# Rank counts placed ahead of a stage's first unit, and seven value tiles halved on VectorE before TensorE sums them

## The reference, cut to what matters

```python
scores = jnp.einsum('tbhd,sbhd->bhts', q, k) * scale     # t, s run over 8 rows
attn = jax.nn.softmax(scores, axis=-1)
ctx = jnp.einsum('bhts,sbhd->tbhd', attn, v)
attn_out = ctx @ out_w.T + out_b
```

```python
position_in_expert = jnp.cumsum(expert_mask, axis=0) - 1
expert_mask = expert_mask * (position_in_expert < capacity)      # capacity 320
...
hidden = jax.nn.silu(xf @ w_gate.T)
combine = (topk_gates[:, :, None] * one_hot(topk_idx)).sum(axis=1)
for e in range(8):
    y = y + combine[:, e:e + 1] * (hidden @ w_down[e].T)
```

## Time and profile before

| | us |
|---|---|
| median of 3 runs | 967.86 |
| lowest and highest | 961.92, 969.95 |
| the profiled execution's own time | 968.87 |
| its span, first to last instruction | 966.7 |
| PE busy in it | 784.6 |
| DVE busy in it | 630.6 |

### The profile page before, as it was taken

How to read it: one execution, slowest core, us unless ns; L and a number is a source line. 1 busy time by engine, 2 the same in 40 slices (tenths; PEclk the granted TensorE clock), 3 DMA queues, 4 the chain that set the end, 5 groups by cost and what they waited for, 6 DMA issues and landing times. The chain is left out here.

```text
span 966.7 us, 14811 instructions
## 1 busy us (share of the span) xinstructions
PE 784.6 (81%) x5019; PEld 536.6 (56%) x5019; DVE 630.6 (65%) x1795; ACT 406.5 (42%) x891; POOL 366.3 (38%) x514
## 2 busy tenths in 40 slices
PE   3667999835888899987988989888879979886374
PEld 1556888623444444444338856656734447665363
DVE  4764322347788888754897747899535869995421
ACT  2043444322666766663360446444220037675210
POOL 6244334077556543301963400111100115554363
PEclk9977999957999999999998979999588989998597
DMA  8605778310000000000000000000100060001310
GB/s 206 240 22 151 215 207 249 115 30 12 13 12 10 9 7 2 1 2 1 0 1 1 1 1 1 1 1 1 66 0 1 0 174 1 23 23 44 86 53 27
DMA packets 52636, 48.60 MB, mean 50 GB/s; under 512 B 6900, under 2 KB 47751, under 8 KB 52306
## 3 DMA queue, kind: packets, MB, share of 16 engines
q1 hardware_dynamic: 49010, 40.06, 13.8%
q0 software_dynamic: 3552, 7.61, 2.9%
HBM read 38.47 MB, written 9.37 MB: 49 GB/s over the span
## 5 line engine op out<-in xcount | busy, mean ns | idle before, releaser
L1735 DVE TENSOR_REDUCE scratch<-psum 128x2 f32<-128x512 f32 (+1 forms) x160 | 106.6, 685 | 39.4 <-PE psum L1442 21.1
L1653 ACT ACTIVATE scratch<-psum 128x512 f32<-128x512 f32 x160 | 94.3, 602 | 67.5 <-PE psum L1462 67.5
L237 POOL TENSOR_SCALAR veps<-moments 128x4 f32<-128x4 f32 (+1 forms) x48 | 10.1, 210 | 290.8 <-DVE moments L158 289.0
L318 ACT ACTIVATE XT<-psum 128x512 f32<-128x512 f32 (+1 forms) x40 | 22.3, 560 | 134.0 <-PE psum L303 133.9
L940 DVE SCALAR_TENSOR_TENSOR scratch<-psum,b_block_bias,scratch 128x256 f32<-128x256 f32 (+1 forms) x48 | 18.6, 430 | 71.6 <-ACT scratch L1104 62.9
L1014 POOL DMA_INDIRECT scratch<-pair_rows,b_gather_at x39 | 39.2, 1006 | 65.0 <-PE psum L1158 42.1
L2562 PE MATMUL psum<-late,scratch 128*128 128x512 f32 x128 | 58.5, 619 | 5.7 <-DVE routing_wide L2508 5.0
L303 PE MATMUL psum<-ident,XN 128*128 128x128 f32 x144 | 29.8, 340 | 32.2 <-DVE XN L169 25.9
L1462 PE MATMUL psum<-scratch,arena 128*128 128x256 bf16 x256 | 49.8, 276 | 5.5 <-ACT scratch L1633 4.4
L240 POOL TENSOR_TENSOR rstd<-veps,minus_half 128x4 f32<-128x4 f32 (+1 forms) x48 | 48.3, 1007 | 6.6
L1442 PE MATMUL psum<-arena 128*128 128x512 bf16 x128 | 50.2, 399 | 0.7 <-DVE scratch L1735 0.6
(11 more groups left out here) (456 smaller groups left out, 2070.7 us busy)
## 6 DMA issues: line engine op xcount, KB each, us to landing
arena<-in_L_ffn_w SPq DMA_DIRECT2D x72, 128.0 KB, 3.1
arena<-in_L_ffn_wg SPq DMA_DIRECT2D x24, 256.0 KB, 3.2
wide<-in_L_xattn_Wkv SPq DMA_DIRECT2D x1, 2048.0 KB
wide<-in_L_ffn_W SPq DMA_DIRECT2D x1, 2048.0 KB, 8.8
late<-in_L_ffn_W SPq DMA_DIRECT2D x8, 256.0 KB, 6.6
pair_results<-scratch SPq DMA_DIRECT2D x15, 128.0 KB, 3.7
folded_values<-arena SPq DMA_DIRECT2D x3, 512.0 KB, 4.9
scratch<-folded_values SPq DMA_DIRECT2D x3, 512.0 KB, 4.6
```

Of the source, the lines that this page charges most:

```text
L1653: a.activation(out, bank[3 + e % 2][:, :], ACT.Exp).then_inc(s["exp"], 1)
L1735: v.tensor_reduce(out, bank[m % 3][:, :].rearrange("p (h t) -> p h t", t=n), AX.X, ALU.max, negate=True).then_inc(s["maxed"], 1)
```

## The change

Two edits, made together.

1. Seven tiles of the value loop, numbers 0, 2, 3, 5, 6 of half 0 and 13, 14 of half 1 (t = 5 and 6), are halved. All are products of DVE. After the product DVE waits for it and adds the buffer's second half (512 numbers) to its first, in place, and only then announces the tile; PE sums four blocks instead of eight.
2. In the capacity stage PE's wait for `chosen` and the two rank matmuls stand behind the gate products, ahead of the wait for `hidden` and of unit 0. The wait for `combine` stays ahead of unit 1.

```diff
+    HALVED = (0, 2, 3, 5, 6, 13, 14)
...
             for t in self.dve_values:
                 k = len(self.dve_values) * m + self.dve_values.index(t)
+                u = 2 + k % 2
                 if k >= 2:
                     v.wait_ge(s["reduced"], self.dve_order[k - 2] + 1)
-                self.value_products(v, m, t, 2 + k % 2).then_inc(s["prod_w"], 1)
+                made = self.value_products(v, m, t, u)
+                if 8 * m + t in self.HALVED:
+                    own.link(v, made)
+                    made = v.tensor_tensor(self.prod[:, u, 0:512], self.prod[:, u, 0:512], self.prod[:, u, 512:1024],
+                                           ALU.add)
+                made.then_inc(s["prod_w"], 1)
...
-                for i in range(8):
+                parts = 4 if 8 * m + r in self.HALVED else 8
+                for i in range(parts):
                     last = t.matmul(c.bank[4 + j // 4][:, (j % 4) * P:(j % 4 + 1) * P],
-                                    self.prod[:, u, i * D:(i + 1) * D], c.ident[:], start=(i == 0), stop=(i == 7))
+                                    self.prod[:, u, i * D:(i + 1) * D], c.ident[:], start=(i == 0),
+                                    stop=(i == parts - 1))
...
+        t.wait_ge(s["chosen"], 1)
+        self.ranks.pe(t, c.routing.table(4).rearrange("p j e -> p (j e)"))
         t.wait_ge(s["hidden"], 2 * NG)
         for q in range(NT // 2):
             if q == 1:
-                t.wait_ge(s["chosen"], 1)
-                self.ranks.pe(t, c.routing.table(4).rearrange("p j e -> p (j e)"))
                 t.wait_ge(s["combine"], 1)
```

## The result

The changed kernel takes 958.03 us (median of 4 runs, 956.72 to 959.45). The ratio to before is 0.9911, 95% interval 0.9888 to 0.9934: 0.7 to 1.1% faster. The forecast was 959.2.

What follows compares the result with a forecast made beforehand. The prediction took PE to bound most stages, and in short gaps whatever PE waits for. Gains of 8.2 (early counts) and 0.45 us (halved tiles) made 8.7, from 967.86 to 959.2 us, range 954.0 to 964.5.

Steps and rivals of the forecast that it cites:

- Part 1: Capacity stage, early rank matmuls: 5.6 us of idle time plus 2.6 of clock, 8.2 us gained, between 6.7 and 9.0.
- clock term: Unit 1 of the capacity stage runs at full clock without the idle time before it: 2.6 us, from 1.7 to 3.4.
- Rival C: Capacity stage: early counts pay only their idle time, as the clock falls elsewhere; 5.6 + 0.45 us, 961.8; chance 0.12.
- so it goes through to the end: After the capacity stage's units: the 8.2 us gained there would last to the kernel's end.
- Part 2: Value loop, seven halved tiles: 28 fewer matmuls save PE some 7 us, but DVE's chain leaves 0.45 us gained.
- PE's idle times: Value loop: PE would stand idle 0.5, 0.9 and 2.6 us before tiles 5, 6 and 8.
- The turns of DVE and POOL: Value loop: DVE and POOL products hold each other up; without that, 1.85 us gained instead of 0.45.
- Rival A: Value loop: the clock falls from tile 8 on after new idle time, costing 0.3 to 2.0 us; about 960.7; chance 0.22.
- signs of being wrong: Unit 0 later than 712.3, a remaining PE wait for `combine`, loop shorter by over 2 us, half-clock between T8 and T15.
- Rival B: Value loop pays in full, DVE's sums being hidden: 6.3 us there, 14.5 with the early counts, 953.4; chance 0.06.
- Rival D: Value loop: PE stays at 1.2 GHz from tile 8 on and beyond; 2.4 us slower, 970.3; chance 0.03.

Runs made afterwards that it cites:

- e3: Kernel before plus five thrown-away products of 128x512 on PE behind the rank matmuls, ahead of the wait for `combine`: 961.56 us against 964.60, ratio 0.9968.
- e1: Early rank counts alone, no tile halved, against the kernel before: 958.08 us against 964.60, ratio 0.9940.
- e8: The changed kernel unaltered, timed again against the kernel before: 956.76 us against 967.91, ratio 0.9890.
- e10: The changed kernel unaltered, timed in another batch against the kernel before: 956.82 us against 964.85, ratio 0.9917.
- e2: The seven halved tiles alone, rank matmuls left behind unit 0, against the kernel before: 964.08 us against 964.60, ratio 0.9992.
- e5: The changed kernel without DVE's seven sums of halves, so part of the output is missing: 952.07 us, one run, no interval.
- e4: The changed kernel with half 1's division split, its reduce and reciprocal ahead of tile 5's product: 956.04 us, ratio 0.9920 to the kernel before.
- both kernels with the delay: Early counts alone plus two thrown-away products (1.7 us) on PE ahead of unit 1, timed twice against the kernel before: ratios 0.9891 and 0.9931.

## Why the prediction was right

**Part 1** was right in its steps, with one term too small. The counts lie in ACT's wait and cost nothing; `combine` is 2.2 us early; units 0 and 1 stand 6.97 us apart instead of 12.55, the 5.6 of the forecast. The clock term was taken at 2.6, between 1.7 and 3.1; in the profile it is the whole 3.1, and e3 shows it alone, 3.0 us between the medians. That makes 8.7 us instead of 8.2. Rival C is partly true: what the clock gives in one stage it takes in another, 2.5 us in the next stage in the profile and 1.7 in e1. The forecast's "so it goes through to the end" missed that.

**Part 2** was right in its mechanism, and in its size where the clock comes back as late as before. The sum takes 0.691 us, the forecast used 0.69. PE's idle times were forecast at 0.5, 0.9 and 2.6 us before tiles 5, 6 and 8 and are 0.34, 0.70 and 2.37; each is 0.16 to 0.23 less. Of that 0.16 is the part of a record (0.275 us) that reaches beyond the start of the next (0.112 us later at 2.4 GHz), which the profile counts as busy and I counted as idle. Tile 8 was to start 0.1 us late against the first product: in e8 it does, in the profile it is 0.8 early, since PE got 2.4 GHz back sooner (7.2 us after the first product instead of 8.9). I had kept the clock's return where it was before: of the 1.1 us of the profile, 0.3 to 0.4 are the halves by the traces of e8 and e10, and the rest is the clock's, which is luck. The turns of DVE and POOL are as forecast in e2, e8 and e10, where PE waits 0.70 us for tile 14.

**Rival A** came to pass in the profile. The clock fell at 526.3, behind the new idle time, and a stretch at 1.2 GHz between tiles 8 and 15 was one of the signs of being wrong. It cost 0.15 us: from tile 8's first record to the projection it was 14.24 us, and 14.09 in e2, e8 and e10, where the clock did not fall there. That is under the rival's 0.3 to 2.0. With PE slower, the waits of 0.70 and 0.15 us before tiles 14 and 11 vanished, as the rival's price had allowed for. (The time that the prediction gives for rival A, 960.7, is not the middle of its own gains of 6.7 to 8.4, which is 960.3.) **Rival B** is excluded by e2; e5 and e4 say why: the sums cost 1.8 us, and the division's place an idle time of 2.4. **Rival D** did not come.

**What the sum did not have** is as large as what it had: 4.8 us gained in stages that the change does not touch, and 4.4 lost. That they nearly cancel is chance, and the forecast's closeness to 958.03 owes something to it. Gains and losses both lie where the stretches at 1.2 GHz differ. The loss in the stage right behind the units is gone in both kernels with the delay; why the clock fell or held elsewhere stays open. So does why the two parts measured alone (0.9940 and 0.9944; 0.9992) come to somewhat less than the change as a whole (0.9911, 0.9890, 0.9917): their intervals don't exclude a plain sum.

## What to carry to other kernels

A small piece of work that stands behind a large one on the busiest engine, while its input has long been there, belongs in a wait that this engine has anyway; the price of the idle time it caused is read twice, as the gap and as the slow unit behind it. Taking work from the bound engine and giving it to the next one pays only as far as the next one's longest dependent chain allows, so look first for what of that chain can be moved into its waits: here each move alone was worth 0.4 us or nothing in the loop, both together 3. And a few products that compute nothing, in a gap that must stay, can be worth their place (3.0 us here), if the engine's clock would fall in that gap.

## What the hardware showed that was not expected

The same work at another moment is granted another clock. The light start of the stage after the units ran the same 26 or 27 records in 4.8 or 4.9 us and was followed by a clock of 0.51 or 1.00, by whether 1.7 us of work had been put ahead of unit 1. Stretches of 20.4 and 30.8 us in all at 1.2 GHz stand at the same place of otherwise equal stages. In this kernel 1.6 to 5.8 us come and go in stages that a change does not touch, even in stages ahead of it; a gain of that size has to be looked for in the trace where it was made, not in the time.
